# Moving the normalisation of the first half's output rows, on VectorE, from the middle of the sixteenth step to behind its gradient transpose

## The reference, cut to what matters

```python
def step(carry, x):
    W1_s, b1_s = carry
    xq, xk, xv, eta_mb = x
    Z1 = xk @ W1_s + b1_s
    grad = _ln_fused_l2_bwd(Z1, xv - xk, ln_w, ln_b)
    Attn1 = jnp.tril(xq @ xk.swapaxes(-1, -2))
    b1_bar = b1_s - jnp.tril(eta_mb) @ grad
    Z1_bar = xq @ W1_s - eta_mb * Attn1 @ grad + b1_bar
    ...
    out = xq + _ln(Z1_bar, ln_w, ln_b)
    return ((W1_new, b1_new), out)
...
_, ys = jax.lax.scan(step, init, xs)
out = ys.transpose(1, 0, 3, 2, 4).reshape(Bb, Ll, HS)
out = _ln(out, post_norm_weight, post_norm_bias)
return out @ o_w.T
...
xn = _layernorm(x, axis=-1)
s = _L0_attn_ref(xn, ...)
g = _silu(_L0_ffn_ref(xn, ...))
x = x + s * g
```

## Time and profile before

| | |
|---|---|
| median of 3 runs | 226.0 us (224.16 to 226.67) |
| the profiled execution | 224.68 us |
| its span, first to last instruction | 222.4 us |
| TensorE busy in the span | 191.9 us (86%) |
| VectorE busy | 193.9 us (87%) |
| GpSimd busy | 154.4 us (69%) |
| ScalarE busy | 114.1 us (51%) |
| mean granted TensorE clock | 0.946 of full speed |

### The profile page before, as it was taken

The page is one execution under the profiler, slowest core; times in us unless marked ns, Lnnn a source line. Parts: engine busy times, 40 slices in busy tenths (PEclk is TensorE's granted clock), DMA queues, the critical chain, the costliest instruction groups (busy, mean ns, idle before and its releaser), DMA issues.

```text
span 222.4 us, 5347 instructions
## 1 busy us (share of the span) xinstructions
PE 191.9 (86%) x1879; PEld 151.7 (68%) x1879; DVE 193.9 (87%) x527; ACT 114.1 (51%) x226; POOL 154.4 (69%) x211
## 2 busy tenths in 40 slices
PE   8523999797899699978997999899799988997991
PEld 6312568254678488957875889689578967876770
DVE  2899999999989999499999999998999999826972
ACT  2372159972636452837265775734825391539420
POOL 2313539999494978695978649989987995764044
PEclk9975799999999889999999999999958996999999
DMA  5995311154593301346033015632400120050004
GB/s 168 362 406 206 94 51 47 13 152 120 137 299 57 104 0 16 73 134 123 9 52 90 3 24 118 120 84 38 113 0 4 21 80 3 0 192 0 0 15 176
DMA packets 40304, 20.59 MB, mean 93 GB/s; under 512 B 23704, under 2 KB 38232, under 8 KB 39768
## 3 DMA queue, kind: packets, MB, share of 16 engines
q1 hardware_dynamic: 38664, 17.83, 30.1%
q10 hardware_dynamic: 1616, 2.44, 3.2%
HBM read 16.79 MB, written 3.44 MB: 91 GB/s over the span
## 4 chain that ended last, share of the span: by engine, by line
PE 37%; DVE 31%; POOL 9%; ACT 9%; issue 8%; DMA 2%; POOLq 1%; SPq 0%; DVEq 0%; ACTq 0%
PE bank L1252 16%; PE bank L1265 7%; PE bank L1293 5%; PE bank L1211 4%; DVE bank L905 3%; PE bank L1279 3%; DVE pr L894 3%; ACT L648 3%; DVE pr L957 2%; DVE dW L962 2%; DMA small<-in_small 2%; POOL hT L389 2%; POOL xqm L373 2%; POOL gate L384 2%; POOL sgpad L408 1%
## 5 line engine op out<-in xcount | busy, mean ns | idle before, releaser
L1252 PE MATMUL bank<-xn_hi,gup_hi 128*128 128x256 f32 x128 | 42.1, 329 | 0.0
L1252 PE MATMUL bank<-xn_lo,gup_hi 128*128 128x256 f32 x128 | 37.6, 294 | 0.0
L1252 PE MATMUL bank<-xn_hi,gup_lo 128*128 128x256 f32 x128 | 37.6, 293 | 0.0
L1265 PE MATMUL bank<-down,hT 128*128 128x256 f32 x128 | 34.6, 396 | 0.7 <-POOL hT L389 0.4
L384 POOL TENSOR_TENSOR gate<-gate,share 128x256 f32<-128x256 f32 x32 | 23.5, 735 | 14.2 <-ACT gate L637 13.5
L321 POOL TENSOR_TENSOR A<-A,mask 128x256 f32<-128x256 f32 x32 | 23.5, 740 | 11.7 <-ACT A L623 11.7
L1211 PE MATMUL bank<-xqm,xkT 32*32 32x128 f32 x512 | 21.1, 279 | 10.2 <-ACT A L623 8.7
L1252 PEld LDWEIGHTS bank<-xn_hi,gup_hi 128*128 128x128 f32 x128 | 25.6, 200 | 5.6 <-issue 4.9
L1252 PEld LDWEIGHTS bank<-xn_hi,gup_lo 128*128 128x128 f32 x128 | 25.9, 202 | 0.5 <-issue 0.2
L1252 PEld LDWEIGHTS bank<-xn_lo,gup_hi 128*128 128x128 f32 x128 | 25.9, 202 | 0.0
L637 ACT ACTIVATE gate<-bank 128x256 f32<-128x256 f32 x32 | 12.3, 385 | 26.2 <-PE bank L1252 25.3
(11 more groups left out here) (165 smaller groups left out, 422.2 us busy)
## 6 DMA issues: line engine op xcount, KB each, us to landing
wblk<-w_blocks SPq DMA_DIRECT2D x8, 512.0 KB, 4.3
share<-shares SPq DMA_DIRECT2D x8, 512.0 KB, 8.6
sgpad<-in_gup SPq DMA_DIRECT2D x1, 1024.0 KB, 9.6
G<-in_gup SPq DMA_DIRECT2D x1, 1024.0 KB, 11.7
down<-in_down SPq DMA_DIRECT2D x1, 1024.0 KB, 14.2
xkT<-in_x_bt SPq DMA_DIRECT2D x1, 1024.0 KB, 5.0
targets<-x_bt ACTq DMA_DIRECT2D x3, 256.0 KB, 4.0
KP<-keys SPq DMA_DIRECT2D x24, 32.0 KB, 2.2
```

Of the source, the lines that this page charges most:

```text
L1252: ins = pe.matmul(bank[4 + i % 2][:, 2 * P * g:2 * P * g + 2 * P], w[:, k, e, NI * g:NI * g + NI].bitcast(F32R), x[:, k, 2 * pair:2 * pair ...
L1265: ins = pe.matmul(bank[7][:, HS * r:HS * r + HS], hT[:, i % 2, P * r:P * r + P], down[:, e, :], start=(e == 0 and r == 0), stop=(e == NE - ...
```

## The change

The two calls of `half_normalise(0, k)` leave the fill at place 1 of the sixteenth step, between the sums and the factors, and stand behind the whole of group 7, thus behind the transpose of its gradients, and ahead of `post_rows(0)`.

```diff
             def first_half_b(m, i):
                 if (m, i) == (0, 1):
                     first_half_stats()
-                if (m, i) == (1, 1):
-                    half_normalise(0, 0)
-                    half_normalise(0, 1)
 
             group(6, 0, first_half_a)
             group(7, 1, first_half_b, last=True)
+            half_normalise(0, 0)
+            half_normalise(0, 1)
             v.wait_ge(S_["small2"], 16)
             post_rows(0)
             post_rows(1)
```

## The result

In the first comparison the changed kernel had a median of 226.02 us (20 runs, 224.42 to 227.63) against 225.76 us for the kernel before (20 runs, 222.14 to 228.45), and a ratio of 1.0065 with a 95% interval of 1.0037 to 1.0093. Taken alone, the ratio says 0.65% slower, some 1.5 us, clear of 1. The prediction said 226.0 us and no change. The ratio leaves out every run more than 1.5% above its kernel's fastest one, which here took 11 of 20 runs from the kernel before (its fastest took 222.14 us, and the median of the nine left is 224.57 us) and none from the changed kernel. Over all 20 and 20 runs the medians give 1.0012, and the means, 225.59 and 226.05 us, are 0.46 us apart with a standard error of 0.37 us, which is not clear of zero.

A forecast was written before the change was run, and what follows sets the result against it. The prediction took TensorE's own gapless queue up to the gradient part L1293 to bound the kernel. All gains and costs were put at 0: 224.68 + 0 = 224.68 us profiled, median unchanged at 226.0 us, range 224.1 to 227.4 us.

The forecast's parts named there:

- How the numbers follow: Weighing of outcomes: same 89%, faster 6%, slower 5%; 1% (2.3 us) taken as distinguishable, since three runs spread by 2.5 us.
- The gradient earlier, for nothing: VectorE's last gradient transpose moves 2.1 us earlier, but GpSimd's padding still starts at 195.88 us: gain 0.
- The bound is TensorE's queue: TensorE runs without idle time from 192.98 us to the gradient part L1293 at 198.87 us; padding is 1.9 us early.
- The moved instructions in their new place: Behind VectorE's transpose they take 2.10 us, from about 192.2 to 194.3 us, covered by the gap before L1041: cost 0.
- VectorE's gap ahead of L1041: Sign in the changed kernel's profile: VectorE still idles 2.4 to 2.9 us before L1041, against 2.83 us before.
- The first two blocks: Normalised blocks for TensorE's transposes L1319: ready at about 193.55 us, 2.8 us early instead of 6.0 us; cost 0.
- Contention: L1051 meeting GpSimd instructions in SBUF, up to three times: 0.45 us on GpSimd, at most 1.64 us, all covered; cost 0.
- the rival by which it is held up: Port lock pushes GpSimd's padding back by 3.3 us and L1293 by 1.4 us, giving 227.4 us; chance 3%.
- the lock of the Trainium skill: VectorE's two-port tensor_scalar and GpSimd share ports exclusively; the second to start blocks. Spoke against the change, sum still 0.
- My argument that L1051 ran at double rate: L1051 took 408 ns for 256 SBUF elements, L1041 402 ns for 128 PSUM elements; offered as support for the port lock.
- The rival of TensorE waiting for the blocks: At L1319, the second block comes at 198.5 us, delaying L1293 and everything behind by 2.1 us: 228.1 us; chance 3%.

The follow-up runs named there:

- Experiment 2: Kernel before with added sums on VectorE behind the sixteenth step's normalisation, delaying the last gradient transpose: ratio 1.0127 with four sums, 1.0041 with two.
- experiment 5: Changed kernel with TensorE's first two transposes of normalised blocks moved from ahead of the bias to behind the gradient part: ratio 1.0028 against the kernel before.
- second comparison: The changed kernel without further edit, timed again against the kernel before: ratio 0.9997 (0.9963 to 1.0032).
- experiment 3: Changed kernel with four added sums (5.6 us) on VectorE between gradient transpose and normalisation: ratio 1.0183 against the kernel before, means 230.36 against 226.07 us.
- experiment 4: Changed kernel with each first-half block normalised twice in the new place, four more reciprocals and four more L1051-like instructions: ratio 1.0067 against the kernel before.

## Why the prediction came out as it did

**No effect.** Over all runs of all comparisons the changed kernel has a mean of 225.81 us (68 runs, standard error 0.13) and the kernel before 225.83 us (149 runs, standard error 0.10). The forecast of no change holds to about 0.3 us, twice the standard error of the difference. The 0.65% of the first comparison did not come back in four further ones (0.9997, 1.003, 0.995, 1.0003).

**Where it failed.** The step that failed is the one on the spread, in "How the numbers follow": I took the 2.5 us between the three runs as a plain margin of measurement that matters only when it carries a ratio past 1%, put the ratio itself at no change, and never asked what made the spread. The runs showed a ratio of 1.0065 with 1 outside its interval and no cost behind it. Most of it comes from which runs the ratio compares, as said with the result: over all of them the medians give 1.0012, and 0.46 us between the means is little more than one standard error. The rest can be the draw of TensorE's granted clock, with which about half of the variance of the times goes (squared correlation 0.44 over 129 runs of the kernel before, 0.50 over 68 of the changed one). Over the recorded runs of these comparisons the kernel before took 226.96 us on the mean where the clock was up to 0.927 (33 runs) and 225.14 us between 0.942 and 0.950 (26 runs); the changed kernel 226.99 us (16 runs) and 225.18 us (20 runs). At equal clock they are the same. Whether the clock had a part in the first comparison stays open: the changed kernel's mean was 0.934 there, and the clocks of the kernel before are not on record. That such a ratio needs no change at all is shown by the copy of the kernel before, which came out at 0.9891.

**The gradient earlier, for nothing: right.** It starts 2.1 us earlier after the sum (2.98 against 5.09 us), as reckoned, and the padding did not move with it. Experiment 2 shows some 3 us of slack and where it ends.

**The bound is TensorE's queue: right up to the gradient part.** The 4.93 us are the same in both kernels, and experiment 5 shortens them by the 0.6 us taken out.

**The moved instructions in their new place: right in kind, too small in size.** I took 2.10 us, from L1048 to the start of L926; to the end of the last L1051 it was 2.19 us. In the new place it was 2.96 us in the first trace (from L1048 at 194.13 us), 3.23 us in the second comparison, and 2.93 to 3.19 us in the other three. VectorE's gap ahead of L1041 shrank from 2.83 us to 1.62 to 1.81 us, where I had expected 2.4 to 2.9 us. The first two blocks were ready at 195.55 us for transposes from 197.97 us, 2.4 us early and not 2.8 us; in the second comparison they were 2.9 us early (193.89 and 196.75 us). The difference is how far VectorE runs ahead of TensorE: from L921 to the last scores it is 5.38 us in the trace of the kernel before, 4.91 us in the first trace of the changed one and 5.34 us in the second. I had also read the wait as one for both blocks. TensorE waits for each by itself, as the order of its instructions shows, and experiment 3 agrees: its transposes started with the first block.

**Contention: right that it is hidden, wrong about who pays.** I put 0.15 us on GpSimd for each meeting and up to 0.41 us each as the end. GpSimd paid 0.04 to 0.05 us (0.77 and 0.78 us in place of 0.73 us), in sum about 0.15 us for three in the first trace and 0.05 us for one in the second; VectorE paid 0.7 to 1.0 us more than in the old place. The padding started 1.94 to 2.13 us after the scores in the five traces of the changed kernel, against 1.94 to 1.99 us before, so the rival by which it is held up falls. The rule that I had named beside it, the lock of the Trainium skill ("SBUF — State Buffer", section "Who interferes with whom"), has the later of the two fully blocked until the other is finished. The traces agree in part. On VectorE's side two L1051 took 1.43 us in place of 0.74 us beside GpSimd, and the 1.18 us of experiment 4 are 0.77 us over the undisturbed 0.41 us, about one instruction of GpSimd. But the L1126 of experiment 4 that started at 194.57 us, with the mask running until 194.92 us, was done at 195.07 us, sooner than 0.41 us behind the mask's end; and GpSimd lost at most 0.07 us on a mask or gate in the new place and 0.15 us in the old one. My argument that L1051 ran at double rate is not shown either: it set an input in SBUF against one in PSUM, and no run separates the two.

**The rival of TensorE waiting for the blocks.** It did not happen in the changed kernel, though in three of its five traces the distance was less than I gave it. Its price may be too low: in experiment 3 2.25 us of wait came with 4.3 us of time, the rest under half clock behind the gap, while in experiment 2 2.67 us came with 2.9 us. Two kernels don't settle what a gap costs beyond itself.

## What to carry to other kernels

Before costing an edit, look for the engine whose queue has no gap up to the point that bounds the end: here the chain of waits ran through GpSimd's padding, while the padding was 1.9 us early. Work moved from one covered place to another was worth nothing here, and only narrowed the slack of the new place. Where the time of one program varies by 1% with the granted clock, compare distances between two rows of the traces, run the old kernel against itself, and look at the mean over all runs and at the clock of each run before believing a ratio of 0.65%.

## What the runs showed of the hardware

The granted clock falls to half in different places from one execution of the same instructions to the next: the gradient part ran at 2.4 GHz throughout in four of nine traces and partly at 1.2 GHz in five, with TensorE's queue unbroken from 188 us on ahead of it in all of them; it cost 1.0 to 1.4 us to the end. I can't say what selects between the two. A gap of 2.25 us in TensorE's queue was followed by 0.53 of full speed from 201 to 208 us, one of 2.67 us (199.5 to 202.1 us) overlapped with 0.50 from 200 to 206 us. And instructions of VectorE and GpSimd that meet in SBUF do not share the loss evenly: L1051 went from 0.41 us to 0.88 and 0.91 us in the changed kernel and to 1.18 us in experiment 4, GpSimd's mask from 0.73 us to at most 0.80 us in the new place and 0.88 us in the old one.
